# Layers stage: the attention rows behind q on VectorE, one product in another form, a subtraction at the end of GpSimd's step

## The reference, cut to what matters

```
x = layernorm(x + attn0(x))                      # first stage
x = layernorm(x + int8_linear(x))                # "y2": rounded to int8, x scale, + bias
q, k, v = x @ wq + bq, x @ wk + bk, x @ wv + bv  # 16 heads of 64, so 1024 columns each
Q, K = elu(q) + 1, elu(k) + 1
KV, Ksum = sum_s(K * v), sum_s(K)                # per column, over the rows of a sequence
Z = 1 / (Q * Ksum + 1e-6)
attn = Q * KV * Z                                # = KV/Ksum * (1 - 1e-6 * Z)
x = layernorm(x + gelu(attn @ wo + bo))          # "y3"
h = x @ w_fc' + rank-16 term;  r = max(h, 0)
x = layernorm(x + (r * r) @ w_proj')             # "y4", the output
```

## Time and profile before

| | us |
|---|---|
| runs of the kernel before | 3335.67, 3339.34, 3342.42 |
| profiled execution | 3338.64 |
| its span, first to last instruction | 3336.8 |
| PE busy in the span | 3050.9 (91%) |
| DVE busy | 2493.3 (75%) |
| ACT busy | 2160.1 (65%) |
| POOL busy | 1671.9 (50%) |

### The profile page before, as it was taken

One profiled execution on the slowest core, in us unless ns is written; L12 is line 12 of the kernel. 1 busy time (PEld: TensorE's weight loads), 2 busy tenths in 40 slices (PEclk: granted clock), 3 DMA queues, 4 the chain that ended last, 5 costly groups with the idle time before them and its releaser, 6 DMA issues. The chain is left out here.

```text
span 3336.8 us, 70306 instructions
## 1 busy us (share of the span) xinstructions
PE 3050.9 (91%) x21167; PEld 2511.4 (75%) x21167; DVE 2493.3 (75%) x6865; ACT 2160.1 (65%) x5664; POOL 1671.9 (50%) x2223
## 2 busy tenths in 40 slices
PE   5999999999999999999999986989888989898886
PEld 4888788778778778778788864777777777777774
DVE  5877787787687787687687766877777777777774
ACT  4766666576576576576576654777767777667764
POOL 4655555455465465465455553344444444444444
PEclk9999999999999999999999997999999999999998
DMA  2000000000000000000000002000000000000000
GB/s 78 8 14 20 9 14 21 9 21 14 15 14 14 15 14 14 15 15 14 16 14 14 20 20 82 14 7 13 14 13 14 13 13 14 13 13 13 7 14 20
DMA packets 50150, 58.70 MB, mean 18 GB/s; under 512 B 2848, under 2 KB 47920, under 8 KB 49472
## 3 DMA queue, kind: packets, MB, share of 16 engines
q1 hardware_dynamic: 47056, 51.78, 4.9%
q10 hardware_dynamic: 2672, 1.87, 0.2%
HBM read 36.86 MB, written 16.78 MB: 16 GB/s over the span
## 5 line engine op out<-in xcount | busy, mean ns | idle before, releaser
L577 POOL TENSOR_SCALAR a_ex<-a_ex,a_rc 128x384 f32<-128x384 f32 (+1 forms) x1024 | 533.8, 535 | 750.0 <-DVE a_rc L489 749.6
L386 ACT ACTIVATE a_ex<-a_sm,a_nm 128x384 f32<-128x384 f32 (+1 forms) x1024 | 572.5, 560 | 100.9 <-DVE a_nm L482 97.9
L482 DVE CUSTOM_DVE_ANT_0 a_sm<-sc,a_mask,a_rn 128x384 f32<-128x384 f32 (+1 forms) x1024 | 532.0, 545 | 46.3 <-PE sc L267 44.2
L392 ACT ACTIVATE a_pt<-tp 128x256 f32<-128x256 f32 (+1 forms) x512 | 220.1, 430 | 305.0 <-PE tp L278 305.0
L236 PE MATMUL pj<-a_whi,a_xhi 128*128 128x384 f32 x1024 | 397.2, 388 | 2.1 <-DVE a_rb L460 2.1
L561 POOL TENSOR_TENSOR a_qr<-a_ra,a_rb 128x256 f32<-128x256 f32 x512 | 367.5, 733 | 36.4 <-DVE a_rb L460 36.4
L1535 POOL TENSOR_TENSOR b_rlo<-b_ring,b_rhi 128x512 fp32r<-128x512 f32 x128 | 171.3, 1338 | 375.5 <-ACT b_rhi L1280 375.4
L267 PE MATMUL sc<-a_kT,a_qT 64*128 64x384 f32 (+1 forms) x2048 | 346.4, 457 | 2.4 <-DVE a_nm L482 0.9
L236 PE MATMUL pj<-a_whi,a_xlo 128*128 128x384 f32 x1024 | 346.1, 338 | 0.0
L236 PE MATMUL pj<-a_wlo,a_xhi 128*128 128x384 f32 x1024 | 345.0, 337 | 0.0
L288 PE MATMUL qk<-a_pt,a_v 128*64 128x128 f32 x5120 | 315.5, 278 | 31.3 <-issue 21.0
(11 more groups left out here) (203 smaller groups left out, 8093.5 us busy)
## 6 DMA issues: line engine op xcount, KB each, us to landing
a_xin<-x SPq DMA_DIRECT2D x16, 512.0 KB, 3.8
a_xres<-x SPq DMA_DIRECT2D x16, 512.0 KB, 3.8
y<-a_res SPq DMA_DIRECT2D x16, 512.0 KB, 3.1
b_y<-y SPq DMA_DIRECT2D x16, 512.0 KB, 3.8
out<-b_y SPq DMA_DIRECT2D x16, 512.0 KB, 2.9
a_xin<-wqkv SPq DMA_DIRECT2D x8, 256.0 KB, 2.7
a_pt<-wqkv SPq DMA_DIRECT2D x1, 1536.0 KB, 6.7
a_ot<-wqkv SPq DMA_DIRECT2D x1, 1536.0 KB, 10.4
```

What stands on the lines that cost most here:

```text
L386: e.activation(ex[h][w][:, 0:width], sm[h][w % 2][:, 0:width], ACT.Exp, bias=nm[:, w, h:h + 1], scale=-1.0, accum_out=rs[:, w, h:h + 1]).t ...
L392: e.activation(pt[0][w][:, 0:width], TP[:, 0:width], ACT.Copy).then_inc(g['pt_act'], 1)
L482: e.tensor_tensor_reduce(out=sm[h][w % 2][:, 0:width], in0=SC[w % 2][h][:, 0:width], in1=mem['mask'][:, off:off + width], scale=rn[:, par, ...
L577: e.tensor_scalar(row, row, 0.0, rc[:, w, h:h + 1], ALU.add, ALU.mult).then_inc(g['exn_pool'], 1)
```

## The change

Four things change, all in the second stage:

1. On DVE, the attention rows (`dve_at`) move from in front of q to behind it, right before the square. The gelu's products, and the statistics of the norms n2 and n4, move from behind q to in front of it.
2. On POOL, the low part of the attention rows (`pool_at_low`) becomes the last work of a step.
3. The -1 and +1 of `dve_q` becomes one tensor_scalar with two constants. Before it was a scalar_tensor_tensor with a second tensor, one column of ones repeated; that column and its memset go.
4. cc and nc have two slots, one for each parity of the sequence, because in step 0 the attention rows of the sequence before are now made behind the sums of the next.

```diff
-        e.memset(mem['one'][:, :], 1.0)
...
     def dve_at(e, s, c):
...
-        factor, term = (mem['nc'][:, c:c + 1], mem['cc'][:, c:c + 1])
+        factor, term = (mem[k][:, s % 2, c:c + 1] for k in ('nc', 'cc'))
...
     def dve_q(e, s, c):
...
-        e.scalar_tensor_tensor(mem['eq'], mem['eq'], -1.0, mem['one'][:, 0:1].to_broadcast([P, S]), ALU.add,
-            ALU.add).then_inc(g['qt_dve'], 1)
+        e.tensor_scalar(mem['eq'], mem['eq'], -1.0, 1.0, ALU.add, ALU.add).then_inc(g['qt_dve'], 1)
...
     def dve_step(e, b, c):
...
             dve_v(e, *kv)
-        if inside(at[0]):
-            dve_at(e, *at)
         if c == 0 and inside(b):
             dve_sums(e, b)
         if c == 0 and inside(b + 1):
             dve_low(e, 'y2h_act', 'y2l_dve', mem['y2lo'][(b + 1) % 2], mem['y2hi'][(b + 1) % 2], b + 1, 0)
-        if inside(b):
-            dve_q(e, b, c)
-        if c == 0 and inside(b + 1):
-            dve_low(e, 'y2h_act', 'y2l_dve', mem['y2lo'][(b + 1) % 2], mem['y2hi'][(b + 1) % 2], b + 1, 1)
         if c == 3 and inside(b - 1):
             for k in range(2):
                 dve_gelu_inner(e, b - 1, k)
...
         if c in (4, 5) and inside(b + 2):
             dve_stats(e, n2, 's2_pool', b + 2, y2_rows(b + 2), c - 4)
+        if inside(b):
+            dve_q(e, b, c)
+        if c == 0 and inside(b + 1):
+            dve_low(e, 'y2h_act', 'y2l_dve', mem['y2lo'][(b + 1) % 2], mem['y2hi'][(b + 1) % 2], b + 1, 1)
+        if inside(at[0]):
+            dve_at(e, *at)
         if inside(b - 2):
             dve_square(e, b - 2, c)
...
     def pool_step(e, b, c):
...
             n3.rstd(e, b - 1)
-        if inside(at[0]):
-            pool_at_low(e, *at)
         if c == 2 and inside(b - 1):
...
             pool_query_weights(e, *query_columns(b, c), c)
+        if inside(at[0]):
+            pool_at_low(e, *at)
```

More of the change, by code:

```diff
@@ L1369, in dve_sums @@
         e.wait_ge(g['v_dve'], HC * s + HC)
-        ks, kb, inv, cc = (mem['su'][:, s % 2, :], *(mem[k][:, :] for k in ('kb', 'ki', 'cc')))
+        ks, kb, inv, cc = (mem['su'][:, s % 2, :], mem['kb'][:, :], mem['ki'][:, :], mem['cc'][:, s % 2, :])
         e.reciprocal(inv, ks)
@@ L1377, in dve_sums @@
         e.wait_ge(g['kv_dve'], 4 * s + 3)
-        e.tensor_scalar(mem['nc'][:, :], cc, -1.0, None, ALU.mult).then_inc(g['kv_dve'], 1)
+        e.tensor_scalar(mem['nc'][:, s % 2, :], cc, -1.0, None, ALU.mult).then_inc(g['kv_dve'], 1)
     def dve_at(e, s, c):
@@ L1636, in layers_memory @@
         DIM], bo=[P, DIM], bias=[P, DIM], psc=[P, DIM], g1=[P, 2, S], g2=[P, 2, S], half=[P, TT],
-        eps=[P, 1], ln_eps=[P, 1], unround=[P, 1], one=[P, 1], xs=[P, 2], top=[P, 2], gate=[P, 1], wst=[P, 4,
+        eps=[P, 1], ln_eps=[P, 1], unround=[P, 1], xs=[P, 2], top=[P, 2], gate=[P, 1], wst=[P, 4,
             FC], nbq=[P, HC],
         nbk=[P, HC], bq=[P, HC], bk=[P, HC], one_bq=[P, HC], one_bk=[P, HC], bv=[P, HC], su=[P, 2, HC], kv=[P, HC],
-        kb=[P, HC], ki=[P, HC], cc=[P, HC], nc=[P, HC], **Norm.buffers('ln2'), **Norm.buffers('ln3'),
+        kb=[P, HC], ki=[P, HC], cc=[P, 2, HC], nc=[P, 2, HC], **Norm.buffers('ln2'), **Norm.buffers('ln3'),
         **Norm.buffers('ln4')).items()}
```

## The result

| | before | changed |
|---|---|---|
| median of 4 runs, us | 3339.43 (3335.67 to 3342.42) | 3225.89 (3224.4 to 3227.37) |
| ratio, 95% interval | | 0.9661 (0.9644 to 0.9677) |
| profiled execution, us | 3338.64 | 3225.97 |
| its span | 3336.8 | 3224.1 |
| 13 steady blocks | 1003.4 (77.2 each) | 900.2 (69.2 each) |

The changed kernel is 113.5 us faster; the forecast was 105 (3234 us). Of the 112.7 us in the span, 103.2 lie in the 13 blocks.

What follows compares the result with a forecast made beforehand. A loop from DVE's square through ACT's functions back to the square was taken to bound it, leaving PE idle 7.6 us a block. 13 x 7.65 plus 5 made 104.5 us less: 3234 us, range 3208 to 3282.

Steps and rivals of the forecast that it cites:

- The tail and the stops: DVE from L1396 to the next rhi shrinks to 2.77 us; alo's stops go, the square's priced at nothing.
- The clean turn of 7.38 us: One undisturbed loop from rhi to rhi: 4.61 us on ACT plus 2.77 on DVE, below PE's 7.9 to 8.0.
- Turn by turn: Count of the loop's eight steps in a steady block: 77.34 us before, 69.25 after, 8.1 less.
- Step 1: Loop turn from 9.40 to 8.4 us; an extra 1.1 us copy stands in front of k on ACT.
- a meeting of an attention row with the gelu work in step 2: In step 2 one attention row may meet POOL's two gelu operations, priced at 0.4 us.
- the count by kinds: Check for a steady block, adding moved work, new form, alo's stops that go and L1374: 7.2 us less.
- Outside the steady blocks: First stage untouched; sequences 0 and 1 gain 1 us together, the block of sequence 15 gains 4: 5 us.
- rival B: PE is the only bound; idle time goes except in steps 0 and 7, block 67 us: 3201 us, chance 0.09.
- rival E: L85 on POOL stops the gelu's product and L1396 in steps 3 and 5, 26 us less gain: 3260 us, chance 0.10.
- A: Stops come back elsewhere, on L1396, L1388 and L1391 beside other POOL work, 47 us less gain: 3281 us, chance 0.13.
- C: Slower: out waits for the later alo and the delay goes round the loop: 3375 us, chance 0.05.
- D: Nothing gained: another wait of the same length replaces the loop at once: 3339 us, chance 0.03.

Runs made afterwards that it cites:

- alo small in the kernel before: Kernel before with alo made for only 8 of its 512 columns from the third unit on, waits and orders unchanged: 3264.72 us, ratio 0.9778.
- the shortened out: Changed kernel without the third of the three products of out (0.47 us of TensorE work a step): 3208.57 us, ratio 0.961.
- the order-only run: Changed kernel with the old two-tensor form of q's first operation put back, new order kept: 3233.32 us, ratio 0.9681.
- the attention-rows-only run: Changed kernel with the gelu's products and statistics put back behind q, behind the attention rows: 3330.4 us, ratio 0.9973.
- The form alone: Kernel before with one edit, L1396 as tensor_scalar with two constants, every order as before: 3307.48 us, ratio 0.9904.
- the small alo in the changed kernel: Changed kernel with alo made for only 8 of its 512 columns from the third unit on: 3226.34 us, ratio 0.9663.
- the other 57: Changed kernel with the attention rows back in front, gelu's products and statistics still in front of q: 3282.57 us, ratio 0.9832.

## Why the prediction was right

**The bound.** Right: v's wait for the square went from 46.7 us to nothing, PE is busy for 97% of the steady part, and its own floor, 7.9 to 8.0 us for a plain step and 8.5 for steps 1 to 3, is what it takes from v to v: 7.95 in steps 4 to 6, 8.40 to 8.47 in steps 1 to 3. Step 2's turn of 7.97 by the rhi rows only looks like the floor of a plain step.

**The tail and the stops.** Right, and shown: alo small in the kernel before takes both long rows away. The square behind the attention rows isn't stopped: no L1407 is over 0.70 us, though more than a third of them start while alo runs (mean of all 685 ns). The clean turn of 7.38 us was 0.3 too short for step 4, which takes 7.67 in the shortened out; TensorE's floor of 7.95 covers that here.

**Turn by turn.** The sum was 69.25, measured 69.42 in the block shown and 69.25 in the mean of 13; the single steps are off by up to 0.4 either way, so the last digits are luck. Step 1 was 0.4 too short: the next rhi, at 2692.20, doesn't wait for the square, which has ended at 2691.77, but stands behind ACT's copy of the eight transposes with which TensorE, never idle here, ends its step. The 0.4 that I gave a meeting of an attention row with the gelu work in step 2 is there: 0.95 us for 0.54 beside L1505. DVE and POOL in step 2 of the changed kernel:

```profile
2697.47 1.33 POOL L1505 TENSOR_SCALAR b_g<-b_g 128x512 f32<-128x512 f32 x2 [3.29 <-ACT b_g L1283]
...
2698.13 0.95 DVE L1387 TENSOR_SCALAR b_ahi<-b_ring,b_nc,b_cc 128x512 fp32r<-128x512 f32 x1
```

**The mean of two counts.** The forecast was 8.2 us too slow, and two terms share that; this one has 3.7 us of it. The turns gave 8.1 us a block, the count by kinds 7.2; I took 7.65, and measured is 7.94. The count by kinds adds what isn't on the path (1.8 us for the form, of which the order-only run shows 0.1) and misses what hangs on it (ACT's gelu functions, as the attention-rows-only run shows). The turns alone would have given 3228 us.

**Outside the steady blocks.** The larger part of the miss, 4.5 us: I gave 5 and it is 9.5. Measured in the two spans: 6.7 us from q of sequence 15 to the end (137.7 to 131.0), and 5.1 from the start of the second stage to q of sequence 2, against 2.3 us that the first stage took longer (its last instruction ends 2004.4 us into the span of the kernel before, earlier than the 2,060 given ahead of the prediction). The last two are no larger than what the profiled kernels differ by there: that stretch takes 181 to 193 us in them, in no order that fits their edits. Only the 6.7 is a gain I would call shown.

**The clock.** Only rival B had a term for it. In the kernel before, the twelve steps 0 of blocks 3 to 14 take 12.42 us at a granted clock of 1.00 (seven) and 13.2 to 13.7 at 0.87 or 0.88 (five); the steps 4 of blocks 2 to 13 take 8.97 at 1.00 (six) and 9.17 to 9.41 at 0.81 to 0.83 (six). In the changed kernel all are at 1.00. So some 7 of the 103 us of the steady blocks are the clock's, an estimate from these differences: 4.9 in steps 0, 2.0 in steps 4. (The form alone has every step 0 at 1.00 too, so some 5 of its 25.6 us are of this kind.) The block of the earlier trace rows has such a slow step 4, so 0.4 of the 1.26 us that I put down to TensorE's floor there was the clock.

**The rule on the shared ports.** The trace of the changed kernel has the very meeting of rival E, a gelu product that starts while L85 runs, POOL and DVE in step 3:

```profile
2703.38 1.02 POOL L85 TENSOR_TENSOR b_ln_rs<-b_ln_ve,b_half 128x4 f32<-128x4 f32 x1
...
2703.93 0.69 DVE L1422 TENSOR_TENSOR b_g<-b_g,b_ring 128x512 f32<-128x512 f32 x1
```

L85 would have held it until 2704.40; it took 0.69 as always. In 11 of the 13 steady blocks L1422 starts while L85 runs, and all 26 of them take 681 to 689 ns. E fails. The Trainium skill (SBUF — State Buffer, "SBUF: two separate sides") has the pair of ports taken for the whole instruction. For 512 columns this case agrees: both forms of q's first operation are held until alo has ended, 63 and 59 times. For L85, with 4 columns in 1.02 us, it doesn't.

**The rivals.** A came true in its mechanism and not in its price: L1387 in step 2, one L1428 a block, L1336 and L1338 are long, 1.8 us in a block together, so the sign that no stopped DVE row would stand beside alo and rlo didn't come. But none is on the loop, where the small alo in the changed kernel gives nothing. Only the meeting in step 2 was priced beforehand; that the other three miss the loop is luck as far as the prediction goes. B was too far: idle time fell to 2.1 us a block, but steps 0 and 7 keep their chains. C and D fail.

## What to carry to other kernels

Follow the loop that ends the waits, turn by turn, and let the sum of the turns stand; a count of saved instruction time by kinds is a check, not a second opinion to be averaged in. A VectorE result that releases a long GpSimd operation is best made last before work that GpSimd doesn't stop, here an operation that reads one tensor from PSUM: the same instructions in another order were worth 3.2%. Test a reordering whole: of the 113 us one half gave 9 and the other 57, each with the new form, which alone gave 32. A faster form of an instruction that is being stopped stays stopped.

## What the runs showed of the hardware that was not expected

- Taking 0.47 us of TensorE work out of each step made the kernel before 0.3% slower; six of step 0's matmuls ran at 0.43 us apart, at the lower clock level, behind an idle gap of 2.15 us instead of 1.69, and all twelve steps 0 were below a granted clock of 1.00 where five were. In the changed kernel the same edit left the clock at 1.00 and gained 17 us.
- The stop works both ways, and the first one there wins: in the attention-rows-only kernel alo took 1.67 us beside L1422, which had started 0.17 us before it, and then held L1424 for 1.40. All 24 alo that started under a gelu product there, from 2190 to 3090 us, took 1.67 to 1.68 us, those that started under the square or the statistics 1.27 to 1.30.
- An operation of 8 columns, 167 ns alone, is held as long as one of 512: L1374 took 1.2 us in each of 13 blocks and ended 0.02 us after alo. An operation of GpSimd with 4 columns, L85, held no row of DVE that started in its 1.02 us.
